# Last stage of a four-layer kernel: where the expert positions are computed, which engine makes the low halves of the weights, and how two norms share a square root

## The reference, cut to what matters

```python
v = var(x);  y = (x - mean(x)) / sqrt(v + 1e-5)               # layer norm
normed = y * rsqrt(mean(y * y) + 1e-8) * norm_weight          # second norm
shared = relu(normed @ sw1 + sb1) @ sw2 + sb2
probs = sigmoid(normed @ router_w.T);  scores, idx = top_k(probs, 2)
w = scores / (sum(scores) + 1e-6)
routed = sum over the 2 chosen experts of w * (relu(normed @ ew1[e] + eb1[e]) @ ew2[e] + eb2[e])
x = x + shared + routed
```

## Time and profile before

| what | us |
|---|---|
| median of three runs | 1502.99 (1501.4 to 1507.45) |
| profiled execution, its own time | 1501.84 |
| span of its core | 1500.0 |
| mean granted TensorE clock | 0.934 of full speed |
| busy: PE, DVE, ACT, POOL | 1261.6, 1012.2, 890.2, 599.2 |

### The profile page before, as it was taken

The page is one execution under the profiler, slowest core; times in us unless marked ns, Lnnn a source line. Parts: engine busy times, 40 slices in busy tenths (PEclk is TensorE's granted clock), DMA queues, the critical chain, the costliest instruction groups (busy, mean ns, idle before and its releaser), DMA issues. The chain is left out here.

```text
span 1500.0 us, 35809 instructions
## 1 busy us (share of the span) xinstructions
PE 1261.6 (84%) x13441; PEld 1047.8 (70%) x13441; DVE 1012.2 (67%) x2018; ACT 890.2 (59%) x1661; POOL 599.2 (40%) x650
## 2 busy tenths in 40 slices
PE   4999998399999999994899999999972576699880
PEld 3777776277877787783798889888962564587760
DVE  5888887576777677764356676767665865576662
ACT  3888887566666666653455566566642455486750
POOL 3222222155555555564223332424121575165561
PEclk9999999599999999997899999999995688799995
DMA  4222221333221332132100000000001221146646
GB/s 140 92 91 93 94 99 50 120 86 92 76 64 45 92 79 69 42 89 75 48 13 17 9 16 9 17 10 9 3 2 42 83 78 35 47 138 222 209 132 181
DMA packets 88083, 109.04 MB, mean 73 GB/s; under 512 B 13290, under 2 KB 54890, under 8 KB 87914
## 3 DMA queue, kind: packets, MB, share of 16 engines
q1 hardware_dynamic: 82922, 96.46, 20.9%
q0 software_dynamic: 4992, 10.30, 2.1%
HBM read 61.11 MB, written 29.82 MB: 61 GB/s over the span
## 5 line engine op out<-in xcount | busy, mean ns | idle before, releaser
L818 POOL TENSOR_TENSOR b_h_lo<-b_h,b_h_hi 128x512 fp32r<-128x512 f32 x168 | 216.6, 1294 | 179.7 <-ACT b_h_hi L842 179.3
L837 ACT ACTIVATE b_zg<-b_zg 128x512 f32<-128x512 f32 x168 | 97.7, 582 | 82.5 <-PE b_zg L882 82.3
L842 ACT ACTIVATE b_h_hi<-b_h 128x512 fp32r<-128x512 f32 x168 | 105.3, 627 | 64.9 <-DVE b_h L1047 64.9
L1047 DVE TENSOR_TENSOR b_h<-b_zg,b_uw 128x512 f32<-128x512 f32 x168 | 116.2, 692 | 32.1 <-ACT b_zg L837 26.8
L1919 POOL DMA_INDIRECT planes_dram<-d_y_out,d_back x92 | 94.2, 1024 | 95.3 <-DVE d_y_out L2227 68.9
L2196 DVE TENSOR_TENSOR d_h_lo<-d_h,d_h_hi 128x512 fp32r<-128x512 f32 x124 | 85.1, 690 | 66.6 <-ACT d_h_hi L1957 32.3
L1040 DVE TENSOR_TENSOR b_uw<-b_zu,b_gw 128x512 f32<-128x512 f32 x128 | 88.2, 689 | 58.0 <-PE b_zu L882 51.3
L1586 DVE TENSOR_TENSOR c_oT_lo<-c_oy,c_oT_hi 128x512 fp32r<-128x512 f32 x64 | 44.1, 689 | 93.7 <-ACT c_oT_hi L1329 93.7
L1246 POOL TENSOR_TENSOR c_prob<-c_prob,c_recip 128x512 f32<-128x512 f32 x64 | 65.5, 1045 | 99.5 <-DVE c_recip L1579 99.5
L318 POOL TENSOR_TENSOR a_qx<-a_qT,headmask 128x256 f32<-128x256 f32 x64 | 37.9, 614 | 150.5 <-ACT a_qT L353 150.5
L525 DVE TENSOR_REDUCE a_top<-a_score_ps 128x8 f32<-128x1024 f32 x64 | 78.1, 1220 | 18.7 <-PE a_score_ps L416 18.7
(11 more groups left out here) (352 smaller groups left out, 4135.4 us busy)
## 6 DMA issues: line engine op xcount, KB each, us to landing
rows_dram<-a_blank SPq DMA_DIRECT2D x32, 520.0 KB, 3.2
b_gw<-gates_dram SPq DMA_DIRECT2D x64, 256.0 KB, 3.7
d_up_slot<-d_up_tab SPq DMA_DIRECT2D x15, 512.0 KB
d_down_slot<-d_down_tab SPq DMA_DIRECT2D x15, 512.0 KB
d_xg<-rows_dram SPq DMA_DIRECT2D x23, 260.0 KB
b_gm<-gates_dram SPq DMA_DIRECT2D x32, 160.0 KB, 3.8
c_craw<-in_c_ctxT_dram SPq DMA_DIRECT2D x16, 256.0 KB, 3.0
d_pay<-planes_dram SPq DMA_DIRECT2D x16, 256.0 KB, 4.6
```

The costliest lines, as they stand in the source:

```text
L818: pool.tensor_tensor(h_lo[:, m % HS, :], h[:, m % HF, :], h_hi[:, m % HS, :].bitcast(F32), ALU.subtract).then_inc(lo_done.sem, 1)
L837: act.activation(zg_ps[:, n % ZG, :], zg_ps[:, n % ZG, :], ACT.Silu).then_inc(sg_done.sem, 1)
L842: act.activation(h_hi[:, m % HS, :], h[:, m % HF, :], ACT.Copy).then_inc(hi_done.sem, 1)
L1047: dve.tensor_tensor(h[:, n % HF, :], zg_ps[:, n % ZG, :], uw[:, n % 2, :], ALU.mult).then_inc(h_done.sem, 1)
```

## The change

The four parts of it are:

1. `finish_stats`: for the two norms together, one square root of (v + 1e-5)·1e-8 + v and one reciprocal, in place of two of each and four small products. It is used with both norms in the last stage alone.
2. `SplitWeights` gets `len(jobs) + 1` for `nth`, so that DVE makes all low halves and POOL none. `share` moves the jobs: one in step -4, two in step -2.0, and the other sixteen over steps 0 to 6 instead of -2 to 4.
3. PE computes the positions of group k+2 in quarter 3 of step k, behind the router of group k+3, instead of those of group k+1 in quarter 1. DVE takes those of group k+1 in quarter 0 instead of 2, and places them in quarter 1 instead of 3.
4. The total count moves from step 7.0 to 6.2 on PE, and DVE's small table of tiles (`tile_map`) from 7.2 to 6.3.

```diff
@@ finish_stats
+        if rms:
+            link(dve.tensor_scalar(tmp[:, 0, :], var[:, :], LN_EPS, 1e-8, ALU.add, ALU.mult))
+            dve.tensor_tensor(tmp[:, 0, :], tmp[:, 0, :], var[:, :], ALU.add).then_inc(asked, 1)
...
         dve.wait_ge(rooted, 1)
-        if not rms:
-            dve.reciprocal(rstd[:, :], root[:, 0, :]).then_inc(ready, 1)
-            return
-        link(dve.reciprocal(rstd[:, :], root[:, 0, :]))
-        link(dve.tensor_tensor(tmp[:, 1, :], rstd[:, :], rstd[:, :], ALU.mult))
-        link(dve.tensor_tensor(tmp[:, 1, :], tmp[:, 1, :], var[:, :], ALU.mult))
-        dve.tensor_scalar(tmp[:, 1, :], tmp[:, 1, :], 1e-8, None, ALU.add).then_inc(asked, 1)
-        dve.wait_ge(rooted, 2)
-        link(dve.reciprocal(root[:, 0, :], root[:, 1, :]))
-        dve.tensor_tensor(rstd[:, :], rstd[:, :], root[:, 0, :], ALU.mult).then_inc(ready, 1)
+        dve.reciprocal(rstd[:, :], root[:, :]).then_inc(ready, 1)
@@ sorted_experts
-        weights = SplitWeights(nc, ctx, tag + "sw", jobs, 3)
+        weights = SplitWeights(nc, ctx, tag + "sw", jobs, len(jobs) + 1)
...
-            if k < -2:
-                return (0, EARLY) if (k, c) == (-START, 0) else (0, 0)
+            if k < 0:
+                return {(-START, 0): (0, PREP_JOBS), (-2, 0): (PREP_JOBS, EARLY)}.get((k, c), (0, 0))
             n, steps = len(jobs) - EARLY, 7 * CH
-            s = min((k + 2) * CH + c, steps)
+            s = min(k * CH + c, steps)
@@ gpsimd
-                weights.rest(pool, *share(k, c), True)
@@ tensor: router(g)
+                pe.wait_ge(logit_done.sem, logit_done.at(g))
@@ tensor: positions(g)
-                pe.wait_ge(logit_done.sem, logit_done.at(min(g + 2, GROUPS)))
@@ tensor: step
-                if 0 <= k + 1 < GROUPS and c == 1:
-                    positions(k + 1)
                 if 0 <= g < GROUPS and c == 3:
                     router(g)
-                if k + 1 == GROUPS and c == 0:
+                if 0 <= k + 2 < GROUPS and c == 3:
+                    positions(k + 2)
+                if k + 2 == GROUPS and c == 2:
@@ vector: step
+                if 0 <= k + 1 < GROUPS and c == 0:
+                    take_positions(k + 1)
...
-                if 0 <= k + 1 < GROUPS and c == 2:
-                    take_positions(k + 1)
...
-                if 0 <= k + 1 < GROUPS and c == 3:
+                if 0 <= k + 1 < GROUPS and c == 1:
                     place(k + 1)
-                if k + 1 == GROUPS and c == 2:
+                if k + 2 == GROUPS and c == 3:
                     tile_map()
```

More of the change, by code:

```diff
@@ L141, in finish_stats @@
     tmp = ctx.enter_context(nc.sbuf_tensor(f"{tag}_tmp", [P, 2, UNITS], F32))
-    root = ctx.enter_context(nc.sbuf_tensor(f"{tag}_root", [P, 2, UNITS], F32))
+    root = ctx.enter_context(nc.sbuf_tensor(f"{tag}_root", [P, UNITS], F32))
     chain = ctx.sem(f"{tag}_stat_steps")
@@ L166, in vector @@
                                       op0=ALU.mult, op1=ALU.add))
-        dve.tensor_scalar(tmp[:, 0, :], var[:, :], LN_EPS, None, ALU.add).then_inc(asked, 1)
-        dve.wait_ge(rooted, 1)
-        if not rms:
-            dve.reciprocal(rstd[:, :], root[:, 0, :]).then_inc(ready, 1)
-            return
-        link(dve.reciprocal(rstd[:, :], root[:, 0, :]))
-        link(dve.tensor_tensor(tmp[:, 1, :], rstd[:, :], rstd[:, :], ALU.mult))
-        link(dve.tensor_tensor(tmp[:, 1, :], tmp[:, 1, :], var[:, :], ALU.mult))
-        dve.tensor_scalar(tmp[:, 1, :], tmp[:, 1, :], 1e-8, None, ALU.add).then_inc(asked, 1)
-        dve.wait_ge(rooted, 2)
-        link(dve.reciprocal(root[:, 0, :], root[:, 1, :]))
-        dve.tensor_tensor(rstd[:, :], rstd[:, :], root[:, 0, :], ALU.mult).then_inc(ready, 1)
+        if rms:
+            link(dve.tensor_scalar(tmp[:, 0, :], var[:, :], LN_EPS, 1e-8, ALU.add, ALU.mult))
+            dve.tensor_tensor(tmp[:, 0, :], tmp[:, 0, :], var[:, :], ALU.add).then_inc(asked, 1)
+        else:
+            dve.tensor_scalar(tmp[:, 0, :], var[:, :], LN_EPS, None, ALU.add).then_inc(asked, 1)
+        dve.wait_ge(rooted, 1)
+        dve.reciprocal(rstd[:, :], root[:, :]).then_inc(ready, 1)
     def scalar(act):
-        for i in range(2 if rms else 1):
-            act.wait_ge(asked, i + 1)
-            act.activation(root[:, i, :], tmp[:, i, :], ACT.Sqrt).then_inc(rooted, 1)
+        act.wait_ge(asked, 1)
+        act.activation(root[:, :], tmp[:, 0, :], ACT.Sqrt).then_inc(rooted, 1)
     return vector, scalar, ready
@@ L2197, in step @@
                                       ALU.subtract).then_inc(lo_done.sem, 1)
+                if 0 <= k + 1 < GROUPS and c == 0:
+                    take_positions(k + 1)
+                    if k + 2 == GROUPS:
+                        dve.tensor_tensor(seen[:, :], seen[:, :].bitcast(F32), in_group[:, :], ALU.add
+                                          ).then_inc(totalled, 1)
                 if 0 <= k + LEAD - 1 < GROUPS and c == 0:
@@ L2205, in step @@
                     x_part(k + LEAD)
-                if 0 <= k + 1 < GROUPS and c == 2:
-                    take_positions(k + 1)
-                    if k + 2 == GROUPS:
-                        dve.tensor_tensor(seen[:, :], seen[:, :].bitcast(F32), in_group[:, :], ALU.add
-                                          ).then_inc(totalled, 1)
-                if 0 <= k + 1 < GROUPS and c == 3:
+                if 0 <= k + 1 < GROUPS and c == 1:
                     place(k + 1)
-                if k + 1 == GROUPS and c == 2:
+                if k + 2 == GROUPS and c == 3:
                     tile_map()
```

## The result

The changed kernel takes 1518.7 us (median of 14 runs, 1512.47 to 1521.53) where the kernel before, measured beside it, takes 1506.15 (1499.38 to 1514.75). The ratio is 1.0072, 95% interval 1.0054 to 1.009: 0.7% slower, some 11 us. A second comparison later gave 1.0084 (1.0055 to 1.0114).

A forecast was written before the change was run, and what follows sets the result against it. No engine is full; a chain of waits sets the pace. Start -3.2, loops +9.4, last group -5.1, stall -8 and clock +6.9 come to 0; late loads' +9.4 on 1501.84 gives 1511 us, range 1499 to 1523.

The forecast's parts named there:

- forecast A: Main forecast: late weights block the tail, first half about even, 1505 to 1516 us; chance 0.48.
- late loads: Tail: two weight loads issued behind the wait for all scatters delay PE's first turn of sorted rows, +9.4 us.
- stall: ACT's unexplained waits for `z`, mostly in step 4, do not come back: -8 us, bounds -9.3 and 0.
- Start: Before the loop: job 1 moves away and POOL stops interfering, so DVE's normalising comes earlier, -3.2 us.
- Low halves on DVE: Five loops, steps -1 to 4: more weight jobs on DVE, +1.5 us, against POOL's interference gone, -1.5.
- Placing: Quarter 1: placing leaves DVE's idle time and stands on the path, 1.55 us per loop, five times, +7.7.
- Positions (and their taking): Quarter 3: positions on PE between router and `z` add +3.0 us over five loops; taking in quarter 0 costs nothing.
- Clock: PE's longer gaps make more steps run at the low clock, 1.15 us each, six times: +6.9 us.
- Last group: Its placing moves from step 6.3 to 6.1: -5.9 us, weight jobs give back 0.8, so -5.1.
- D: Rival, faster: PE's 27.6 us of waits before the router fall by half or more, 1491 us; chance 0.07.
- E: Rival: the weights' lateness is hidden by other work or the loads pass the wait, +0, 1502 us; chance 0.05.
- C: Rival: the stall stays or returns elsewhere and the clock is low, +17, 1519 us; chance 0.25.

The follow-up runs named there:

- fillers: Changed kernel with its last two weight loads ahead of the scatter wait, plus 24 unread PE matmuls before the router in steps 0 to 4: ratios 1.0022 and 0.9991.
- second trace of the kernel before: The kernel before, unchanged, profiled once more on the second chip: one execution, 1479.72 us.
- loads-ahead kernel: Changed kernel with only its last two weight loads issued on SP ahead of the wait for all scatters: 1508.86 us, ratio 1.0011; again 1507.58, 1.0003.

## Why the prediction was right

The forecast was +9.4 us over the profiled execution, 1511 us in a range of 1499 to 1523; measured are 1518.7 and a ratio that is worth 10.8 us. The change in time is forecast A's. The time itself is above A's own range (1505 to 1516), mostly because the kernel before came out at 1506.15, 4.3 us above the execution that I added to.

In whole, by the ratios of the first chip: the late loads cost 9.2 us (12.2 the second time), the third part 11.6 (8.7), and the rest of the change gives back 9.9 (8.3), each with an uncertainty of some 5 us. The forecast had 9.4 for the loads, 11.2 for the third part (placing, positions, the filled wait, the last group's two quarters, clock), and -11.2 for the rest, of which -8 is the stall. Point by point, by the marks:

- **Start, -3.2 forecast.** `x_lo` of group 1 came 2.9 us earlier, with and without the third part. The parts were off: normalising began 1.2 earlier, not 2.4, since with job 1 gone another wait of 1.2 us stood ahead of it, and its eight instructions ended 2.3 earlier. By `x_lo` of group 2 only 1.6 were left (4.5 without the third part): the first placing and a wait for the first positions stand in that loop, which I had not counted.
- **Square root, 0.** Shown, by its own run.
- **Low halves on DVE, 0 in the sum.** The cost and the gain that I set against each other both exist, and DVE's busy time stayed the same. I had read the median of 340 ns as a sign that most of DVE's work escaped POOL; a median hides single instructions, and all six subtractions held one up. What I had left out is the wait for ACT's high halves: alone, the move costs 5.2 us over five loops and 4 us in the end. How much of it is in the change, with its jobs at other times, was not measured by itself.
- **Placing, +7.7.** Measured 6.7 over the five loops by moving it back, and 8.4 with the first placing. That it is on the path is shown; the size is a lower bound, as the kernel with the placing moved back had 18.5 us more of unresolved waits.
- **Positions (and their taking), +3.0.** From the placing in quarter 3 to the kernel without the third part it is 5.0 us by `x_lo` of group 7, in one pair of traces of which the first has the unresolved waits. The low clock doubles them to 1.07 us a step, as the earlier trace rows allowed, and lifts the rest of the way as well.
- **Clock, +6.9; stall, -8.** The granted clock fell to 0.72. The loops with the clock at 1.00 were 2.7 and 2.9 us shorter than the same loops without fillers, more than the 1.15 that I had read from one path in the earlier trace rows. The stall's share is the one part that came out by luck: ACT's unresolved waits up to 1300 were 8.1 us before and none after (the 3.3 us in the table of waits come behind 1370), but no run tells what brings them, and the second chip has none at all. Together, from group 2 to group 7, I had 9.4 - 8 + 6.9 = +8.3; measured 78.9 - 70.6 = +8.2. Against the trace without a stall, on the other chip, it is 78.9 - 63.2 = 15.7, where I had 9.4 + 6.9 = 16.3. Some errors cancel in that.
- **Last group, -5.1.** From `x_lo` of group 7 to the last placing it was 26.5 us and is 22.7: -3.8. In the second trace of the kernel before it is 20.8, so this gain holds against the first trace only.
- **Late loads, +9.4.** Measured 12.1 and 9.5 us between the request and the turn (14.95 and 12.30 against 2.84), in the two traces of the changed kernel. The parts of the first: the landing and the high half began at 1290.61, 4.49 after the request, where I had 2.84 + 0.5; to the first `down` 2.10; to the turn 8.36 where I had 7.5, 0.74 of it a wait for DVE, whose table of tiles stands ahead of `x_resid`. In the second trace the clock rose on the way, and the turn came 6.79 us after the `down`. My 9.4 leaves out the 0.5 us for the landing and counts the 0.77 us of a turn that was there before; the two nearly cancel. Its lower bound takes 3 x 0.47 = 1.41 us for an `up` at the high clock, no less than the 1.42 at the low one; in the changed kernel one at the high clock takes 0.81 (1301.78 to 1302.59). By the eighth tile 2.8 us of the distance to the kernel before are gone, but 2.1 are so in the loads-ahead kernel too: right behind its first turn the kernel before ran at a clock of 0.68 (1286 to 1300), that one at 0.88. In time the late loads were worth 9.2 and 12.2 us in two comparisons.

Of the rivals, D (the 27.6 us of waits really fall) is refuted: the wait grew, because `x_lo` is what ends it. E (hidden) is refuted by the loads-ahead kernel. C has the low clock in every step in common with A; what tells them apart is the stall, and it did not return, so it was A, although 1518.7 is C's number. In the changed kernel PE's gaps ahead of the routers of steps 0 to 3 are 6.0, 6.0, 4.4 and 4.7 us, and the granted clock of the four loops is 0.71, 0.71, 0.70 and 0.70; in the second trace of the kernel before they are 3.2, 2.9, 3.3 and 3.7 us, and 0.87, 0.87, 0.84 and 0.77. TensorE's rule in the Trainium skill (TensorE: Matmul & The Clock Gate, HAM oscillation), that idle gaps let the clock fall again in each iteration, agrees with these rows.

Of the signs that I gave, one came only in half: five of PE's eight waits ahead of the router are under the 5 us that I named. ACT's wait for the load (16.8 us), the clock (0.72), the period of steps 1 to 3 (16.1 to 16.8 us) and the first scatter, 5.7 us earlier, came as stated; the first turn came later than stated, 12.1 us behind the old distance.

Left open: what holds `z` back from ACT on the first chip, and whether the changed kernel avoids it or was spared twice; how the change does on the second chip; and whether a piece of the loss lies behind the eighth tile, where both traces of the changed kernel (170.0 and 172.7 us) are longer than the others of that chip (162.3 to 169.7).

The change without its third part and with its loads ahead is the fastest on the first chip in both lots, 0.66% and 0.55% under the kernel before. Its last mark there (186.0 us) is still 3.2 behind the kernel before on the second chip (182.8), so part of that win may be the stall that it avoids.

## What to carry to other kernels

Before moving work later, look at each in-order queue for a wait that the moved instructions would fall behind; here two loads behind a wait for scatters cost 9 to 12 us, and one edit on the queue gave it back. The engine named in a wait is the last to come, not the only one late: the releaser named was moved away, and the next one was 0.1 us behind it. A piece of work moved to another engine brings its own wait along: the low halves cost DVE no busy time, but 5 us of waiting for their high halves. An instruction that sits in another engine's shadow is free only there, and lengthening the matmul engine's pause cost twice here, as its clock was low behind the longer pauses.

## What the runs showed of the hardware

The same kernel took 1505 us in two lots and 1482 us in a third, with spreads of 1496.37 to 1518.43 against 1479.29 to 1486.69. Between one trace of each, 22.1 us apart, 10.5 lie in the stage up to the eighth tile, where the slower one has 8.1 us of unresolved waits, 9.0 behind it (163.2 against 154.2 us), and 2.6 in the stages before; what causes them is open. Ratios near 1 from different lots should not be set against each other. 24 matmuls that nobody reads, in PE's pause, made two of four loops 2.7 and 2.9 us shorter (the second of them only on the second chip, set against a loop of the first), with the clock at 1.00 in place of 0.71 and 0.70, and the kernel as a whole not measurably. And a GpSimd subtraction of 128x512 held up one VectorE instruction each time, by 0.3 to 1.3 us, six times in one kernel.
